# Transposing the normalised tokens on VectorE in the expert stage of a one-core Mamba and mixture-of-experts kernel

## The chip, the cores and the metric

The kernel runs on one core of one Trainium2 chip. The metric is device time in microseconds for one launch, the median of several runs. The core's engines are TensorE (matmuls and transposes, results in PSUM), VectorE, ScalarE and GpSimd (elementwise work), and SyncE, which issues the DMAs. Each engine works through its own list of instructions in order, and semaphores tie the lists together.

## What is computed

The input has 4 sequences of 1024 tokens with 128 channels in fp32. A Mamba block comes first (layer norm, projection, convolution, selective scan over 64 states, gate, output projection, residual), then a layer norm. Behind it stand four mixture-of-experts layers, and a last residual and layer norm:

```python
logits = jnp.einsum('bsh,he->bse', x, rw) + rb
vals, idx = jax.lax.top_k(softmax(logits), K)          # K = 2 of E = 4 experts
vals = vals / vals.sum(axis=-1, keepdims=True)
xhat = (x - mu) * rsqrt(var + EPS)
xe = xhat[None] * g[:, None, None, :] + b[:, None, None, :]
h = gelu(einsum('ebsh,ehf->ebsf', xe, w1) + b1)        # F = 512
y = einsum('ebsf,efh->ebsh', h, w2) + b2
out = sum over e of comb[e] * (x + y[e])
```

## The kernel before

The first part of the kernel is the Mamba block; its scan fills VectorE until about 1346 us. The expert stage follows. It computes all four experts for all tokens and weights them. Its unit is a group of GT = 4 tiles of 128 tokens. There are NG = 8 groups in a layer and NL = 4 layers, so 32 groups, numbered n = 0 to 31; g is the number within the layer, gp the parity that chooses one of two buffers.

Each engine has a function `step(layer, g, gp, new, more, scale, split)` that emits its work for one group, and `run_layers` calls it for each of the 32. The order within an engine is the order of the calls in its `step`:

- TensorE: `first(n, ., ., e)` computes the hidden block of expert e, 4 blocks of 3 matmuls with 512 columns (L1352), from `xhT`, the transposed normalised tokens, kept as an upper part and a remainder. It rotates over three PSUM banks, so the fourth block needs a bank that ScalarE's GELU has read. `second(n, ., e)` multiplies by w2, 32 matmuls (L1364). The order is first 0, first 1, second 0, `stage_xh(n + 1)` (four transposes of the next group's tokens into PSUM, L1331), first 2, second 1, first 3, second 2, second 3. In the last step of a layer `bias_of_offset` (L1340, 32 matmuls with one column) stands between first 0 and first 1; it waits for the last `add_expert` of the step before (semaphore `f_sum`), since its result goes to the same PSUM bank. The first step of a layer waits behind first 0 for all of the layer's split weights (`f_wp`).
- ScalarE: the GELUs of the four experts (L1109), and ahead of those of expert 2 `stage_norm(n + 2)`: it centres (L1083) and scales (L1089) the tokens of the group after next into `xhs`. It waits for VectorE's moments and for GpSimd's root.
- VectorE: `stage_moments(n + 2)` (L1418 to L1660), `start_sum(n)` (L1726), `add_expert` of expert 0 (L1736, reads PSUM), in the last layer `finish_moments(g - 1)` (it begins with L1762), `split_xh(n + 1)` (L1744 casts the transposed tokens from PSUM to `xhT`, L1746 takes the remainder), `stage_scores(n + 1)` (L1670 to L1677), in a layer's last step `add_bias`, `add_expert` of expert 1, in the last layer `finish_norm` (L1649), `stage_router(n + 1)` (L1682 to L1709), `add_expert` of expert 2, in the steps g = 2, 4, 6 and 7 of layers 0 to 2 `split_w1` (L1624, L1627, for the next layer), `sum_bias(n + 1)` (L1716, L1719), `add_expert` of expert 3.
- GpSimd: the root of the variances (L708), the products of `stage_scores` (L846), in the last layer the root for `finish_moments`, the exponents (L838, between VectorE's scores and its router), the weighted biases (L855, between VectorE's router and `sum_bias`).

Group 0's and group 1's tokens are transposed at other places than the rest; `begins` marks step 0.

Of the kernel before, what the change touches and what calls it, by code (L numbers as in the profile page):

```python
# [11 lines left out]
P = 128  # L12
# [28 lines left out]
GT = 4  # L41
# [3 lines left out]
def build(nc, x, vecs, chan, taps, a_log, ident, w_in, w_xproj, w_dt, w_out,  # L45
          router_w, router_b, ln_g, ln_b, w1, b1, w2, b2, out):
    fp32 = mybir.dt.float32
    bf16 = mybir.dt.bfloat16
    fp32r = mybir.dt.float32r
    ALU = mybir.AluOpType  # L50
# [13 lines left out]
    with ctx:  # L64
# [3 lines left out]
        def sem(name):  # L68
            return ctx.enter_context(nc.semaphore(name))
# [34 lines left out]
        at_, space, limit = [0], [arena], [ARENA]  # L104

        def shaped(v, shape):
            if len(shape) == 2:
                v = v.rearrange("p (a b) -> p a b", b=shape[1])
            elif len(shape) == 3:
                v = v.rearrange("p (a b c) -> p a b c", b=shape[1], c=shape[2])  # L110
            elif len(shape) == 4:
                v = v.rearrange("p (a b c d) -> p a b c d", b=shape[1], c=shape[2], d=shape[3])
            return v

        def carve(n):

            at_[0] += n
            assert at_[0] <= limit[0], at_[0]
            return space[0][:, at_[0] - n:at_[0]]

        def take(*shape):
            return shaped(carve(int(np.prod(shape))), shape)
# [29 lines left out]
        FRONT_END = at_[0]  # L152
# [84 lines left out]
        xhT = parts_xh[:].rearrange("p (g w t) -> p g w t", g=2, w=2)  # L237
# [6 lines left out]
        xhs = take(2, GT, P)  # L244
# [24 lines left out]
        b1_s = take(NL * E * GT)  # L269
        at_[0] = USZ_AT  # L270
        xsum_o = take(GT, H)
        at_[0] = BST_AT
        usz_last = take(2, HALVES, 2, TC)
        xres_last = carry[:, 0, 0:H]
# [87 lines left out]
        f_xhT = sem("f_xhT")  # L362
        f_xhTs = sem("f_xhTs")
# [15 lines left out]
        f_xhu = sem("f_xhu")  # L379
# [5 lines left out]
        f_xn = sem("f_xn")  # L385
# [11 lines left out]
        FIN0, LG0, XH0 = 1, 1, 1  # L397
# [101 lines left out]
        def xh_bank(n):  # L499
            return 4 if isinstance(n, int) and n == 0 else 5  # L500
# [621 lines left out]
        def _(pe):  # L1122
# [51 lines left out]
            for k in range(ITEMS):  # L1174
# [3 lines left out]
                for h in range(HALVES):  # L1178
                    last = nc.tensor.matmul(PS[0:N + R, 4 * bb, :], wx_s[:, h, 0:N + R], u_s[bb][:, h],
                                            start=(h == 0), stop=(h == 1))  # L1180
# [6 lines left out]
                for h in range(HALVES):  # L1187
                    last = nc.tensor.matmul(PS[:, 4 * bb + 2 + h, :], wdt_s[N:N + R, h * P:(h + 1) * P],
                                            dtr_s[bb][N:N + R, :], start=True, stop=True)
# [7 lines left out]
                for t in range(TT // P):  # L1197
                    for h in range(HALVES):
                        last = nc.tensor.matmul(PS[:, 4 * bb + 1, t * N:(t + 1) * N],
                                                u_s[bb][:, h, t * P:(t + 1) * P], wx_s[:, h, N + R:],  # L1200
                                                start=(h == 0), stop=(h == 1))
# [65 lines left out]
            def project(m):  # L1267

                pe.wait_ge(g_done, m + 1)
                if held(m) and not (isinstance(m, int) and m == NCH - 1):  # L1270
                    pe.wait_ge(post_done, m)
                for h in range(HALVES):
                    last = nc.tensor.matmul(projected(m), G[:, h], wout_s[:, h], start=(h == 0),
                                            stop=(h == 1 and in_end(m)))
                if not in_end(m):
                    for r in range(2):
                        last = nc.tensor.matmul(projected(m), ident_s[:], xres, start=False, stop=(r == 1))
                last.then_inc(out_ready, 1)
# [48 lines left out]
            def stage_xh(n, gp):  # L1327

                pe.wait_ge(f_xn, n + 1)
                for s in range(GT):  # L1330
                    last = nc.tensor.transpose(PS[:, xh_bank(n), s * P:(s + 1) * P], xhs[:, gp, s], ident_s[:])  # L1331
                last.then_inc(f_xhT, 1)
# [11 lines left out]
            def first(n, lp, gp, e):  # L1344


                for c in range(GT):
                    i = E * GT * n + GT * e + c

                    pe.wait_ge(f_gelu, i + (3 if e == c == 0 else 1))  # L1350
                    for part_w, part_x in ((0, 0), (0, 1), (1, 0)):
                        last = nc.tensor.matmul(PS[:, HIDDEN[(GT * e + c) % 3], :],  # L1352
                                                w1p[:, lp, part_w, e, c * P:(c + 1) * P],
                                                xhT[:, gp, part_x],
                                                start=(part_w + part_x == 0), stop=(part_w == 1))
                    last.then_inc(f_h, 1)
# [21 lines left out]
            def step(layer, g, gp, new, more, scale, split):  # L1378
                l, pair, lp = layer
                n = l * NG + g  # L1380
                starts = isinstance(g, int) and g == 0
                if starts:
                    pe.wait_ge(f_wp, l * E + 1)
                pe.wait_ge(f_xhTs, n + 1)
                first(n, lp, gp, 0)
                if starts:
                    pe.wait_ge(f_wp, l * E + E)
                if isinstance(n, int) and n == 0:
                    project(NCH - 1)
                if new:  # L1390
                    bias_of_offset(*new, n)
                begins = isinstance(n, int) and n == 0
                first(n, lp, gp, 1)
                second(n, lp, 0)
                if more and not begins:
                    stage_xh(n + 1, 1 - gp)
                first(n, lp, gp, 2)
                second(n, lp, 1)
                first(n, lp, gp, 3)
                if begins:  # L1400
                    stage_xh(1, 1)
                second(n, lp, 2)
                if isinstance(n, int) and n == 0:
                    pe.wait_ge(p_link, (NCH - 1) * P_LINKS + 1)
                if new:
                    pe.wait_ge(f_bias, new[0] + 1)
                second(n, lp, 3)

            run_layers(pe, begin, step)


        @block.vector
        def _(dve):
# [74 lines left out]
            for k in range(ITEMS):  # L1488
# [8 lines left out]
                for h in range(HALVES):  # L1497
                    last = nc.vector.tensor_scalar(rl[bb][:, h], PS[:, 4 * bb + 2 + h, :], chan_s[:, h, KC + 1:KC + 2],
                                                   0.0, ALU.add, ALU.max)
# [154 lines left out]
            def stage_moments(n, g):  # L1654

                dve.wait_ge(f_sum, E * n + E)
                if held(n):
                    dve.wait_ge(f_xn, n)
                moments(f_moments, n * 2, lambda s: at(X, g, s), st_f, mv_f, rs_f, GT, f_var)
                nc.vector.tensor_scalar(nm_f, mv_f[:, :, 0], -1.0, None, ALU.mult).then_inc(f_neg, 1)  # L1660
# [69 lines left out]
            def add_expert(n, g, gp, e):  # L1730
# [7 lines left out]
                                                          ALU.mult, ALU.add)  # L1738
                last.then_inc(f_sum, 1)

            def split_xh(n, gp):

                dve.wait_ge(f_xhT, n + 1 + XH0)
                nc.vector.tensor_copy(xhT[:, gp, 0], PS[:, xh_bank(n), :]).then_inc(f_xhu, 1)  # L1744
                dve.wait_ge(f_xhu, n + 1)
                nc.vector.tensor_tensor(xhT[:, gp, 1], PS[:, xh_bank(n), :], xhT[:, gp, 0].bitcast(fp32), ALU.subtract).then_inc(f_xhTs, 1)  # L1746
# [86 lines left out]
            def step(layer, g, gp, new, more, scale, split):  # L1833
                l, pair, lp = layer
                n = l * NG + g
                next_l, _, next_lp = new or layer
                if more:
                    stage_moments(n + 2, (g + 2) % NG)
                start_sum(n, g, gp)
                begins = isinstance(n, int) and n == 0  # L1840
                add_expert(n, g, gp, 0)
                if last_layer(l) and not (isinstance(g, int) and g == 0):
                    finish_moments(g - 1)
                if more:
                    if not begins:
                        split_xh(n + 1, 1 - gp)
                    stage_scores(n + 1, next_l)
                if new:
                    add_bias(next_l, next_lp)
                add_expert(n, g, gp, 1)  # L1850
                if last_layer(l) and not (isinstance(g, int) and g == 0):
                    finish_norm(g - 1, 1 - gp)
                if more:
                    stage_router(n + 1, 1 - gp)
                if begins:
                    split_xh(1, 1)
                add_expert(n, g, gp, 2)
                if split:
                    split_w1(*split)
                if more:  # L1860
                    sum_bias(n + 1)
                if not (last_layer(l) and isinstance(g, int) and g == NG - 1):
                    add_expert(n, g, gp, 3)
# [51 lines left out]
```

## Time and profile before

| | |
|---|---|
| Median of 3 runs | 2208.34 us (2207.08 to 2210.01) |
| The profiled execution | 2209.82 us, of which its span from first to last instruction is 2208.2 us |
| Granted TensorE clock, mean | 0.983 |
| Busy share of the span | TensorE 97%, its weight loads 58%, VectorE 83%, ScalarE 73%, GpSimd 42% |

The busy shares are means over the scan and the expert stage, in which different engines are busiest. The rows below come from one profiled execution; times in them are microseconds from the start of the span, and a duration called mean is in nanoseconds.

### The profile page before, as it was taken

What the parts mean: (1) busy time and instruction counts of PE and PEld (TensorE: products, weight loads), DVE (VectorE), ACT (ScalarE), POOL (GpSimd) and SP (SyncE); (2) the same over time, 40 slices, a digit from 0 to 9 for tenths busy, and PEclk for the clock granted to TensorE, in tenths of its full rate; (3) what the DMA queues carried; (4) which work ended last, traced back from release to release, by engine and by line L of the source; (5) the groups of instructions that cost most, each with busy time, mean ns of one, the idle gap of its engine ahead of it and who ended that gap; (6) DMA issues with size and microseconds to landing.
All of it is one profiled execution on the core that took longest, in us unless ns stands there. A gap on an engine that the chain in (4) does not pass through costs nothing.

```text
span 2208.2 us, 50669 instructions
## 1 busy us (share of the span) xinstructions
PE 2133.7 (97%) x17080; PEld 1270.6 (58%) x17080; DVE 1833.8 (83%) x2721; ACT 1617.4 (73%) x2160; POOL 926.1 (42%) x453
## 2 busy tenths in 40 slices
PE   7978999999999999999999998999999999999998
PEld 3432333333333333333333336899999999999997
DVE  6879999999999999999999997666565556556775
ACT  5878999999999999999999995445455455545453
POOL 3124344444444444444444333544444444444542
PEclk9978999999999999999999999999999999999999
DMA  5994212121212122222222134000100010000000
GB/s 172 299 281 133 49 41 48 40 48 40 48 40 47 40 47 42 45 44 44 45 42 46 41 86 149 1 0 0 39 1 0 0 39 1 0 1 2 14 10 15
DMA packets 354957, 114.93 MB, mean 52 GB/s; under 512 B 283000, under 2 KB 345600, under 8 KB 354624
## 3 DMA queue, kind: packets, MB, share of 16 engines
q1 hardware_dynamic: 350416, 110.92, 20.0%
q10 hardware_dynamic: 4464, 3.02, 0.4%
q8 instruction: 44, 0.72, 0.1%
q14 instruction: 33, 0.27, 0.0%
HBM read 67.98 MB, written 45.88 MB: 52 GB/s over the span
## 4 chain that ended last, share of the span: by engine, by line
PE 41%; DVE 29%; issue 23%; SPq 3%; ACT 2%; POOL 1%; DVEq 1%; DMA 0%; ACTq 0%; POOLq 0%
DVE arena L1588 25%; PE PS L1364 20%; PE PS L1352 16%; PE PS L1249 1%; ACT behind L981 1%; SPq L519 1%; SPq L615 1%; SPq L521 1%; PE PS L1232 1%; ACT behind L971 1%; PE PS L1331 1%; PE PS L1219 1%; PE PS L1340 1%; DVE arena L1431 0%; PE PS L1142 0%
## 5 line engine op out<-in xcount | busy, mean ns | idle before, releaser
L1588 DVE TENSOR_TENSOR_SCAN arena<-behind 128x1040 f32<-128x1040 f32 x512 | 1153.8, 2308 | 14.3 <-ACT behind L981 10.6
L1109 ACT ACTIVATE arena<-PS,arena 128x512 f32<-128x512 f32 x512 | 344.6, 688 | 405.8 <-PE PS L1352 405.3
L971 ACT ACTIVATE behind<-PS 128x1024 f32<-128x1024 f32 x512 | 526.4, 1028 | 100.7 <-DVE arena L1588 52.5
L1249 PE MATMUL PS<-arena 128*32 128x128 f32 x8192 | 566.2, 406 | 0.0
L981 ACT ACTIVATE behind<-PS 128x1024 f32<-128x1024 f32 x512 | 540.0, 1055 | 16.4 <-PE PS L1232 9.4
L1364 PEld LDWEIGHTS PS<-arena 128*128 128x128 f32 x4096 | 473.2, 192 | 7.7
L1364 PE MATMUL PS<-arena 128*128 128x128 f32 x4096 | 473.5, 275 | 0.0
L791 POOL COPY behind<-carry 128x64 f32<-128x64 f32 x128 | 212.9, 1664 | 508.2 <-ACT carry L998 266.8
L1249 PEld LDWEIGHTS PS<-arena 128*32 128x32 f32 x8192 | 234.9, 119 | 287.5 <-issue 211.3
L1352 PE MATMUL PS<-parts_xh,parts_w 128*128 128x512 f32 x1536 | 383.4, 401 | 9.5 <-ACT arena L1109 6.5
L1736 DVE SCALAR_TENSOR_TENSOR arena<-PS,arena 128x128 f32 (+1 forms) x508 | 142.8, 343 | 258.3 <-PE PS L1364 257.2
L1232 PE MATMUL PS<-arena 96*128 96x512 bf16 x1024 | 313.9, 389 | 42.0 <-ACT behind L981 14.3
L1352 PEld LDWEIGHTS PS<-parts_xh,parts_w 128*128 128x128 f32 x1536 | 284.2, 191 | 68.5 <-ACT arena L1109 10.3
L1219 PE MATMUL PS<-arena,Ast 96*128 96x512 bf16 x1024 | 313.9, 389 | 2.9 <-ACT behind L971 2.7
L1232 PEld LDWEIGHTS PS<-arena 96*128 96x128 bf16 x1024 | 68.8, 98 | 247.2 <-ACT behind L981 216.8
L1219 PEld LDWEIGHTS PS<-arena,Ast 96*128 96x128 bf16 x1024 | 58.7, 98 | 229.4 <-ACT behind L971 184.5
L838 POOL TENSOR_TENSOR arena<-euler,arena 128x16 f32<-128x16 f32 x32 | 92.6, 2895 | 166.1 <-DVE arena L1677 165.9
L846 POOL TENSOR_TENSOR arena<-arena 128x2048 f32<-128x2048 f32 x32 | 145.6, 4551 | 12.3 <-POOL arena L708 12.3
L855 POOL TENSOR_TENSOR arena<-arena 128x2048 f32<-128x2048 f32 x32 | 115.6, 3612 | 78.1 <-DVE arena L1707 78.1
L708 POOL TENSOR_TENSOR arena<-arena,neg_half 128x4 f32<-128x4 f32 (+1 forms) x50 | 50.7, 1014 | 226.7 <-DVE arena L1426 226.6
L805 POOL COPY arena<-arena 64x64 f32<-64x64 f32 x64 | 130.1, 2032 | 11.8 <-POOL behind L791 9.7
L717 POOL TENSOR_SCALAR arena<-arena 128x1 f32<-128x1 f32 x32 | 60.2, 1883 | 151.4 <-DVE arena L1562 151.4
(139 smaller groups left out, 1433.4 us busy)
## 6 DMA issues: line engine op xcount, KB each, us to landing
dl_d<-arena SPq DMA_DIRECT2D x48, 256.0 KB, 3.5
du_d<-arena SPq DMA_DIRECT2D x48, 256.0 KB, 3.5
arena<-dl_d SPq DMA_DIRECT2D x512, 24.0 KB
arena<-b_d SPq DMA_DIRECT2D x64, 192.0 KB
arena<-du_d SPq DMA_DIRECT2D x512, 24.0 KB
b_d<-arena SPq DMA_DIRECT2D x48, 128.0 KB, 2.4
u_d<-behind SPq DMA_DIRECT2D x8, 512.0 KB, 3.9
sz_d<-arena SPq DMA_DIRECT2D x8, 512.0 KB, 4.7
```

The source lines that it names most:

```text
L791: nc.gpsimd.tensor_copy(seg(dB[:, G_])[:, :, 0], carry[:, pair, d:d + GD]).then_inc(slot_ready, 1)
L846: nc.gpsimd.tensor_tensor(scored, X[:, bass.ds(g * GT, GT), :].unsqueeze(2).broadcast_to([P, GT, E, H]), rw_s[:, bass.ds(l, 1)].broadcast_ ...
L971: nc.scalar.activation(seg(dA[:, half])[:, :, 1:], PS[:, 0:2, :].rearrange("p j (i t) -> p (j i) t", t=TC), ACT.Exp).then_inc(exp_done, 1)
L981: nc.scalar.activation(seg(dB[:, G_])[:, :, 1 + 2 * OCT * r:1 + 2 * OCT * (r + 1)], PS[:, 2:4, :].rearrange("p o (t d) -> p d (o t)", d=GD ...
L1109: nc.scalar.activation(hT[:, e % 2, c], PS[:, HIDDEN[(GT * e + c) % 3], :], ACT.Gelu, bias=bias1[:, lp, e * GT + c:e * GT + c + 1]).then_i ...
L1219: last = nc.tensor.matmul(PS[:, j, :], Ast[0:ROWS, kk * (DB // GI) + 2 * q + j, :], rhs_d[kk][0:ROWS, 2 * q + j].rearrange("r i t -> r (i ...
L1232: last = nc.tensor.matmul(PS[:, 2 + oct_ % 2, :], Bst[kk][0:ROWS, oct_, :], rhs_u[kk][0:ROWS, oct_, :, G_ * GD:(G_ + 1) * GD], start=True, ...
L1249: last = nc.tensor.matmul(PS[32 * j:32 * j + 32, 4 + kk, 0:DB], cd[:, pair, j, 32 * i:32 * i + 32], seg(hb[kk])[:, :, 1 + 16 * j + i], sta ...
L1352: last = nc.tensor.matmul(PS[:, HIDDEN[(GT * e + c) % 3], :], w1p[:, lp, part_w, e, c * P:(c + 1) * P], xhT[:, gp, part_x], start=(part_w ...
L1364: last = nc.tensor.matmul(PS[:, y_bank(n, e, s), s * P:(s + 1) * P], hT[:, e % 2, c, s * P:(s + 1) * P], w2_s[lp][:, e * GT + c], start=(c ...
L1588: nc.vector.tensor_tensor_scan(hb[kk][:, q * QD * SEG:(q + 1) * QD * SEG], dA[:, q % 2], dB[:, G_, lo:lo + QD * SEG], 0.0, ALU.mult, ALU.a ...
L1736: last = nc.vector.scalar_tensor_tensor(at(X, g, s), PS[:, Y_BANK[e], s * P:(s + 1) * P], comb[:, gp, s * E + e:s * E + e + 1], at(X, g, s ...
```

## The change

In the expert stage the tokens of groups 2 to 31 are no longer transposed by TensorE. VectorE does it at the place where it has so far split the transposed tokens, in the step of the group before: 16 instructions, each of which takes 32 partitions and 4 x 32 elements, transposes the four 32x32 blocks in them and writes them to another set of 32 partitions of a new tile `xh_turned` in SBUF. The cast and the remainder then read that tile and not PSUM. The step's wait for ScalarE's normalised tokens (`f_xn`) moves from TensorE to VectorE. Groups 0 and 1 keep TensorE's transposes, and so does the code of `split_xh` for them.

```diff
         at_[0] = USZ_AT
         xsum_o = take(GT, H)
+        at_[0] = FRONT_END
+        xh_turned = take(GT, P)
...
                 second(n, lp, 0)
-                if more and not begins:
-                    stage_xh(n + 1, 1 - gp)
                 first(n, lp, gp, 2)
...
+            def turn_and_split(n, gp):
+
+                dve.wait_ge(f_xn, n + 1)
+                dve.wait_ge(f_xhTs, n)
+                for i in range(4):
+                    for j in range(4):
+                        last = nc.vector.transpose(xh_turned[32 * j:32 * j + 32, :, 32 * i:32 * i + 32],
+                                                   xhs[32 * i:32 * i + 32, gp, :, 32 * j:32 * j + 32])
+                last.then_inc(f_xhT, 1)
+                dve.wait_ge(f_xhT, n + 1 + XH0)
+                whole = xh_turned.rearrange("p s t -> p (s t)")
+                nc.vector.tensor_copy(xhT[:, gp, 0], whole).then_inc(f_xhu, 1)
+                dve.wait_ge(f_xhu, n + 1)
+                nc.vector.tensor_tensor(xhT[:, gp, 1], whole, xhT[:, gp, 0].bitcast(fp32), ALU.subtract).then_inc(f_xhTs, 1)
...
                     if not begins:
-                        split_xh(n + 1, 1 - gp)
+                        turn_and_split(n + 1, 1 - gp)
                     stage_scores(n + 1, next_l)
```

## Rows read from the trace of the kernel before

**Rows 1.** Chain that ended last, from 1330 us on: shares of lines.
```profile
by line: PE PS L1364 50.3%; PE PS L1352 39.6%; PE PS L1331 1.6%; PE PS L1340 1.3%; PE PS L1249 1.2%; issue 0.7%; POOL arena L838 0.7%; POOL arena L846 0.5%; POOL arena L855 0.4%; PE PS L1287 0.4%; POOL arena L708 0.3%; DVE arena L1418 0.3%;
```

**Rows 2.** Timeline of TensorE (PE), one group of layer 0: start, duration, instructions.
```profile
1444.62 3.73 PE L1364 MATMUL PS<-arena 128*128 128x128 f32 x32
1448.18 0.60 PE L1331 MATMUL PS<-ident_s,arena 128*128 128x128 f32 x4
...
1451.37 3.73 PE L1364 MATMUL PS<-arena 128*128 128x128 f32 x32
...
1457.68 7.30 PE L1364 MATMUL PS<-arena 128*128 128x128 f32 x64
1464.74 5.70 PE L1352 MATMUL PS<-parts_xh,parts_w 128*128 128x512 f32 x24
1470.28 3.73 PE L1364 MATMUL PS<-arena 128*128 128x128 f32 x32
```

**Rows 3.** Timeline of VectorE (DVE), the same stretch; in brackets idle time before.
```profile
1448.47 1.13 DVE L1736 SCALAR_TENSOR_TENSOR arena<-PS,arena 128x128 f32 x4 [4.78 <-PE PS L1364]
1449.51 0.68 DVE L1744 CAST parts_xh<-PS 128x512 fp32r<-128x512 f32 x1
...
1456.74 0.17 DVE L1682 TENSOR_REDUCE arena<-arena 128x4 f32<-128x16 f32 x1 [0.39 <-POOL arena L838]
...
1462.78 1.22 DVE L1716 TENSOR_TENSOR arena<-arena 128x1024 f32<-128x1024 f32 x1
...
1465.24 1.12 DVE L1736 SCALAR_TENSOR_TENSOR arena<-PS,arena 128x128 f32 x4 [0.51 <-PE PS L1364]
1466.28 0.86 DVE L1418 BATCH_NORM_STATS2 arena<-arena 128x6 f32 x4
...
1467.90 1.18 DVE L1726 SCALAR_TENSOR_TENSOR arena<-arena 128x128 f32 x4
```

**Rows 4.** Timeline of GpSimd (POOL), the same stretch.
```profile
1453.82 2.89 POOL L838 TENSOR_TENSOR arena<-euler,arena 128x16 f32<-128x16 f32 x1 [5.27 <-DVE arena L1677]
1459.14 3.61 POOL L855 TENSOR_TENSOR arena<-arena 128x2048 f32<-128x2048 f32 x1 [2.43 <-DVE arena L1707]
```

**Rows 5.** Groups of VectorE instructions (busy us, mean ns); L1624: shortest, median, longest ns.
```profile
L1418 DVE BATCH_NORM_STATS2 arena<-arena 128x6 f32 x92 | 19.8, 277 | 0.0
L1482 DVE TENSOR_TENSOR arena<-arena 128x128 f32<-128x128 f32 x1 | 0.3, 293 | 0.0
L1726 DVE SCALAR_TENSOR_TENSOR arena<-arena 128x128 f32 x92 | 26.4, 345 | 0.7 <-issue 0.3
L1624 DVE CAST parts_w<-arena x12: 415/422/672, 1436.7 to 1993.1; - x9, 128x512 fp32r<-128x512 f32 x3
```

**Rows 6.** Timelines of ScalarE (ACT) and TensorE in step 0.
```profile
1370.10 1.28 ACT L1083 ACTIVATE arena<-arena 128x128 f32<-128x128 f32 x4 [7.42 <-DVE arena L1660]
...
1373.31 1.65 PE L1352 MATMUL PS<-parts_xh,parts_w 128*128 128x512 f32 x3 [5.73 <-ACT arena L1109]
```

**Rows 7.** L1639's durations (shortest, median, longest ns), and GpSimd beside the longest.
```profile
L1639 DVE COPY arena<-arena x2: 228/1838/3447, 1350.5 to 1363.1; 128x128 f32<-128x128 f32 x2
...
1362.73 3.70 POOL L855 TENSOR_TENSOR arena<-arena 128x2048 f32<-128x2048 f32 x1 [2.59 <-DVE arena L1707]
```

**Rows 8.** Timelines of VectorE and TensorE at the end of layer 0.
```profile
1542.97 1.12 DVE L1736 SCALAR_TENSOR_TENSOR arena<-PS,arena 128x128 f32 x4
...
1544.81 4.42 PE L1340 MATMUL PS<-lb_s,arena 128*128 128x1 f32 x32
```

**Rows 9.** Last layer: L1762's durations, ends of two moments, GpSimd's products between.
```profile
L1762 DVE TENSOR_TENSOR arena<-arena x7: 680/1315/2256, 2031.5 to 2185.5; 128x512 f32 x6, 128x512 f32<-128x512 f32 x1
...
2077.40 0.16 DVE L1660 TENSOR_SCALAR arena<-arena 128x4 f32<-128x4 f32 x1
2103.41 0.16 DVE L1660 TENSOR_SCALAR arena<-arena 128x4 f32<-128x4 f32 x1
...
2079.03 4.58 POOL L846 TENSOR_TENSOR arena<-arena 128x2048 f32<-128x2048 f32 x1 [0.46 <-POOL arena L708]
```

## The prediction, made before the changed kernel was run

> **What bounds the kernel now.** I read the chain that ended last first, then the timelines of single groups in the expert stage. The stage runs from about 1346 us to the end, 32 groups in four layers, and the change touches nothing else. There the chain is TensorE almost alone: half of it in L1364, 40% in L1352, and the transposes of L1331 hold 1.6% [rows 1]. A group of layers 0 to 2 takes TensorE 25.66 us without a gap, 1444.62 to 1470.28 [rows 2]. So whatever leaves TensorE shortens the stage, as long as no other engine's loop over one group becomes longer than TensorE's.
>
> The second reading is VectorE's loop, because its order is fixed in `step`. Its idle time looks large (4.78 us before the first `add_expert` of a group, [rows 3]), but not all of it is free. Follow one round: first add 1448.47, then the split, the scores, GpSimd's exponent 1453.82 to 1456.71, router 1456.74, GpSimd's weighting to 1462.75, `sum_bias` 1462.78, last add 1465.24, moments until 1467.90 [rows 3, 4]. VectorE works in order, so it can't use its waits for GpSimd for what stands behind them. Whatever is put between the first add and the scores pushes all of this back, one for one.
>
> **What is removed.** TensorE loses four transposes in each of 30 groups. With them, second() and the first() behind it take 1444.62 to 1451.37, 6.75 us; without, 1451.37 to 1457.68, 6.31 us [rows 2]. 0.44 us a group, 30 x 0.44 = 13.2 us, all on the path; a group becomes 25.22 us. VectorE's cast now reads SBUF and not PSUM: 0.42 us by L1624 [rows 5] for the 0.68 of L1744 [rows 3], 0.26 less.
>
> **What is added: T.** Sixteen VectorE instructions of 32 partitions x 128 elements, in front of that cast. No row shows this operation. The nearest make one pass over 128 elements per partition. L1418: 277 ns each [rows 5], but four in 0.86 us [rows 3], so they overlap and follow at (0.86 - 0.277) / 3 = 0.195 us. L1482: 293 ns, and L1726: 345 ns [rows 5]. Bounds: all overlapped, T = 16 x 0.195 = 3.1 us; none overlapped, at the slowest row, T = 16 x 0.345 = 5.5. I take L1482's duration without overlap, T = 16 x 0.293 = 4.7 us: successive instructions go to other partitions here, so I don't count on the overlap of rows that stay on theirs.
>
> The Trainium skill ("VectorE: DVE Perf Modes", "Two Vector instructions with no wait between them") states that an instruction starts only when all earlier ones have finished if its output starts in another quadrant than the last output; here it does so every time. No row of this trace shows it. The same page ("The three transpose paths") gives 311 ns for a pass over 128 elements, by which T would be 5.0 us and the sum below some 6 us more (an estimate), and its rules send a 128x128 transpose to TensorE. It speaks against this change.
>
> **Where T lands in layers 0 to 2.** Times from t0, when TensorE begins first() of expert 2 (1448.18 in [rows 2]; there the transposes stand first). First add at +0.29; to the exponent 5.35 (1448.47 to 1453.82) less 0.26, plus T; to the router 2.92; router and weighting 6.04; `sum_bias` 1.95 (2.46 to the last add, less its 0.51 idle); last add and moments 2.66 [rows 3, 4]. Sum 18.95 + T = 23.65, against 25.22 to the next t0: moments end 1.57 us ahead of it. Their reader is ScalarE's normalisation, which stands in front of the GELUs of expert 2. Step 0 of this trace shows that chain failing: ScalarE, idle 7.42 us until VectorE's L1660, starts at 1370.10, and TensorE goes on at 1373.31 after 5.73 us idle [rows 6]. So TensorE's fourth hidden block needs the moments 3.3 us earlier, and it begins 2.1 us after t0 (three quarters of 2.8). Room: 1.57 + 2.1 - 3.3 = 0.4 us. An ordinary group still gains its 0.44.
>
> Two places have no room. (a) Four steps of a layer (g = 2, 4, 6, 7) run split_w1 behind the third add. Its cast copies from SBUF to SBUF, and such a copy waits out a GpSimd operation: L1639 ran 228 ns once and 3447 ns beside GpSimd's L855, which ended at 1362.73 + 3.70 = 1366.43 [rows 7]. VectorE now gets to that cast while L855 runs, so split_w1's 1.15 us fall behind it and into the loop: 0.4 - 1.15, a stall of 0.75 us in the step after g = 2 and after g = 4, 6 x 0.75. After g = 7 TensorE meets it earlier, at the wait for f_wp behind the next layer's first(0): it is there at 1464.74 - 1448.18 - 0.44 + 2.8 = 18.9 us after t0, the split ends at 18.95 + T - 1.95 - 2.66 + 1.15 = 20.2: 3 x 1.3. Together 8 us. (b) In a layer's last step TensorE's bias_of_offset waits for the last add of the step before. Now that add begins at 1542.97 and is over at 1544.0, and L1340 starts at 1544.81 [rows 8]. After, it is over at 18.95 + T - 1.62 (moments) + 1.15 = 23.2, and TensorE is there at 18.9 again. Stall 4.3 us, three times: 13 us. It takes in the stall after g = 6.
>
> **The last layer.** Here finish_moments stands in front of the split, and its L1762 reads two SBUF tiles while GpSimd's L846 runs: 680 ns at best, 2256 at worst [rows 9]. From moments to moments it is 2077.40 to 2103.41, 26.01 us [rows 9], longer than TensorE's 25.66 already. The idle time before the first add is not in this loop: it goes by L846, which ends at 2083.61, and L1762 behind it. So T counts whole: 26.01 - 0.26 + 4.7 = 30.45 us, 5.2 longer than 25.22. Moments end 1.6 us before t0 in step 25 and 3.6 behind it in step 26, where the stall is 3.6 + 3.3 - 2.1 = 4.8; then 5.2 in each of steps 27 to 30: 25.6 us. (Steps 24 and 31 have no such work.)
>
> The Trainium skill ("SBUF — State Buffer", "Reading the diagram") calls the port pair of VectorE and GpSimd an exclusive lock; L1639 and L1762 agree. If it did not bear on split_w1, the sum would be some 12 us less (8 of a, 3 x 1.15 of b; an estimate).
>
> **The sum.** -13.2 + 8 + 13 + 25.6 = +33.4 on this execution's 2209.8 (span 2208.2, 1.6 around it): 2243.2. It is 1.5 above the median of 2208.3, so I forecast **2242 us**, 1.5% slower.
>
> The ends. T = 3.1: no stall in (a), 3 x 2.7 in (b), last layer 1.7 + 4 x 3.6 = 16, sum -13 + 8 + 16 = +11, 2219. T = 5.5: nearly every step of layers 0 to 2 is short (some 13 us), 3 x 5.1 in (b), 5 x 6.0 in the last layer: +45, 2253. TensorE is slower behind a stall: three matmuls took 1.65 us after step 0's [rows 6], where twelve take 2.8 elsewhere. In the last layer VectorE's loop hides that; in (b) it can add some 1.5 us each, 5 in all, which I leave to the range.
>
> **Rivals.**
> 1. The sixteen overlap, T 3.1 to 4.2: 2219 to 2232. For it: small VectorE instructions without a wait between them overlap in this trace. Against: none of them changes its partitions.
> 2. They are slower than any row, since a transpose fills before it drains: 0.39 us each, T = 6.2. Then VectorE's loop without any wait for TensorE (1.18 start_sum + 18.66 + 6.2 = 26.0) is longer than 25.22 in layers 0 to 2 too: +60, 2268.
> 3. The other side, faster: T fits the slack. The point is T = 2.0: (b) 3 x 1.6, last layer some 10 us with its first two steps free, sum +1. At T = 1.3 (0.08 us each) (b) 2.7, last layer 5.6: -5, 2203. Against: even L1418, with overlap, follows at 0.195.
> 4. VectorE's loop in the last layer is not the bound and no bias stall comes: 2195 to 2200. Against it stands that 26.01 is measured and that L1762's wait grows.
>
> **Chances.** The forecast, T 4.2 to 5.5: 0.62. Rival 1: 0.18. Rival 2: 0.11. Rival 3: 0.05, half of it faster by over 0.2%. Rival 4: 0.04. A measurement of this kernel tells 0.2% (4.4 us) from no change. Faster 0.06, same 0.03, slower 0.91. The likeliest case alone gives 2230 to 2258 with the clock's 5 us; the range reaches down to T = 3.1 and up between T = 5.5 and 6.2: 2218 to 2264.
>
> **What would show it.** Right: only 8 of L1331's 128 left; a burst of sixteen that takes 4.2 to 5.5 us; 25.2 us a group in layers 0 to 2 where nothing stalls; TensorE idle before L1340 until VectorE's add, some 4 us, three times; in the last layer TensorE idle before L1352, released by ScalarE's L1109, some 5 us in five steps that last 30.4 us. Wrong: a burst under 2.1 or over 6 us; L1762 not held by L846; split_w1's cast not held by L855; or TensorE waiting for xhT itself, which in this account is ready some 9 us early, and 3 in the last layer.

## The result: 2264.5 us, 2.6% slower, half a microsecond above the forecast's range

The changed kernel takes 2264.47 us (median of 6 runs, 2263.41 to 2267.92) against 2209.11 for the kernel before (6 runs): a ratio of 1.0256, 95% interval 1.0243 to 1.0269. The forecast was 2242 us in a range of 2218 to 2264. The direction and each place of the loss came as said; the sum was 33 us where 55 came, and the measured time lies just outside the range.

The page of the changed kernel, its chain by engine and the group of the new instructions (busy us, mean ns):

```profile
PE 2144.5 (95%) x16960; PEld 1272.2 (56%) x16960; DVE 2013.3 (89%) x3201; ACT 1613.1 (71%) x2160; POOL 927.1 (41%) x453
DVE 37%; issue 36%; POOL 13%; PE 7%; SPq 3%; ACT 2%; DVEq 1%; DMA 0%; POOLq 0%; ACTq 0%
L1747 DVE STREAM_TRANSPOSE arena<-arena 32x128 f32<-32x128 f32 x480 | 145.9, 304 | 6.2
```

TensorE has 120 matmuls fewer, and its 41% of the chain of the kernel before has become 7%: the chain now runs through VectorE and the GpSimd operations that its loop waits for. ("issue" in the second row is time in which an engine waited for nothing that the profile shows.) The new instructions last 304 ns each. Line numbers of TensorE, ScalarE and GpSimd are two higher than before (L1354 is first(), L1366 second(), L1342 bias_of_offset, L848 and L857 GpSimd's products).

VectorE's timeline in step 27 of the changed kernel (last layer), and GpSimd's beside it, answer to [rows 3] and [rows 9]:

```profile
2118.65 0.16 DVE L1660 TENSOR_SCALAR arena<-arena 128x4 f32<-128x4 f32 x1
2118.81 1.14 DVE L1726 SCALAR_TENSOR_TENSOR arena<-arena 128x128 f32 x4
2120.15 1.12 DVE L1736 SCALAR_TENSOR_TENSOR arena<-PS,arena 128x128 f32 x4 [0.20 <-DVE arena L1726]
2121.19 4.18 DVE L1777 TENSOR_TENSOR arena<-arena 128x512 f32 x1
...
2126.92 5.08 DVE L1747 STREAM_TRANSPOSE arena<-arena 32x128 f32<-32x128 f32 x16
2132.04 0.43 DVE L1752 CAST parts_xh<-arena 128x512 fp32r<-128x512 f32 x1
```

```profile
2120.29 4.53 POOL L848 TENSOR_TENSOR arena<-arena 128x2048 f32<-128x2048 f32 x1 [0.46 <-POOL arena L710]
```

The reader is to see three things. The burst takes 5.08 us and is followed at 2132.04, so T is 5.1 and not 4.7. L1777, which was L1762, takes 4.18 us because it ends only behind L848 (2124.82). And VectorE no longer waits for TensorE before the first add: the row at 2120.15 has 0.20 us of idle time, and not behind TensorE, where the kernel before had 4.78 us in layer 0 ([rows 3]) and 2.65 us in a step of the last layer (before its row at 2107.48).

TensorE's timeline in the changed kernel, in steps 3 and 5, at the end of layer 0, in the step behind it, and in the last layer, in the order of time:

```profile
1451.30 0.97 PE L1354 MATMUL PS<-parts_xh,parts_w 128*128 128x512 f32 x3 [0.38 <-ACT arena L1111]
...
1503.06 0.97 PE L1354 MATMUL PS<-parts_xh,parts_w 128*128 128x512 f32 x3 [0.82 <-ACT arena L1111]
...
1550.04 6.96 PE L1342 MATMUL PS<-lb_s,arena 128*128 128x1 f32 x32 [4.59 <-DVE arena L1736]
1556.86 5.47 PE L1354 MATMUL PS<-parts_xh,parts_w 128*128 128x512 f32 x12
...
1586.30 3.06 PE L1354 MATMUL PS<-parts_xh,parts_w 128*128 128x512 f32 x12 [1.43 <-DVE parts_w L1627]
...
2091.43 1.65 PE L1354 MATMUL PS<-parts_xh,parts_w 128*128 128x512 f32 x3 [5.43 <-ACT arena L1111]
...
2100.09 7.30 PE L1366 MATMUL PS<-arena 128*128 128x128 f32 x64
...
2122.18 1.65 PE L1354 MATMUL PS<-parts_xh,parts_w 128*128 128x512 f32 x3 [3.70 <-ACT arena L1111]
...
2130.84 7.30 PE L1366 MATMUL PS<-arena 128*128 128x128 f32 x64
```

These are the stalls that the prediction named: at the fourth hidden block (0.38, 0.82, then 5.43 and 3.70 in the last layer), before bias_of_offset (4.59), and at the wait for the split weights (1.43). No stall of another kind appears in steps 2 to 31. The new thing is the length of the rows behind them: 6.96 us for the 32 narrow matmuls that took 4.42 in [rows 8], and 5.47 for twelve matmuls of first(). The windows of that stretch (length, then busy us and counts of TensorE, its weight loads, VectorE, ScalarE and GpSimd, then the granted clock, of which 1.00 is 2.4 GHz, then the DMA):

```profile
1545.00:1548.00 3.00, 0.45 (x2) 0.02 (x1) 2.75 (x3) 1.78 (x3) 0.77 (x1) 1.00 0.00 0
1548.00:1551.00 3.00, 0.96 (x5) 0.99 (x5) 2.81 (x13) 0.00 (x0) 0.00 (x0) 0.61 0.00 0
1551.00:1554.00 3.00, 3.00 (x16) 3.00 (x15) 1.48 (x10) 0.00 (x0) 2.28 (x2) 0.50 0.02 5
```

TensorE was idle from 1545.4 to 1550.0; the clock was granted at half, 1.2 GHz, from within that time on, and it stayed there through the narrow matmuls.

The kernel before had such a stretch too, without any idle time. Its windows of TensorE at the same place (length, busy us and count, granted clock), behind the 32 narrow matmuls of [rows 8]:

```profile
1547.00:1550.00 3.00, 3.00 (x15) 0.57 0.01 3
1550.00:1553.00 3.00, 3.00 (x8) 0.50 0.00 0
```

Measured by the start of each group's 64 matmuls of second(2) and second(3) in both traces, the 55.1 us divide as follows. The forecast's column is its own sum, with the 0.44 us of removed work counted where it falls.

| part | forecast | measured |
|---|---|---|
| steps 0 and 1 | -0.4 | +0.5 |
| 21 steps: 19 of layers 0 to 2 (without layer ends), and steps 24 and 25 | -1.2 | +2.9 |
| the three layer ends (39.42, 38.44, 39.34 us; before 32.46, 30.86, 29.27) | +11.7 | +24.6 |
| steps 26 to 30 (32.48, then 30.75 to 30.80 us; before 25.69) | +23.4 | +27.1 |
| sum | +33.4 | +55.1 |

### The profile page after: what moved, and what is told of

The parts are those of the page before. It is cut to its first block, busy times and chain, and to the rows that moved or that the text cites. A ratio compares the mean times of both kernels' runs of the same rounds, so it can differ in the third digit from the quotient of the medians.

```text
span 2263.3 us, 50927 instructions
## 1 busy us (share of the span) xinstructions
PE 2144.5 (95%) x16960; PEld 1272.2 (56%) x16960; DVE 2013.3 (89%) x3201; ACT 1613.1 (71%) x2160; POOL 927.1 (41%) x453
## 4 chain that ended last, share of the span: by engine, by line
DVE 37%; issue 36%; POOL 13%; PE 7%; SPq 3%; ACT 2%; DVEq 1%; DMA 0%; POOLq 0%; ACTq 0%
DVE arena L1588 25%; POOL arena L848 5%; POOL arena L840 4%; POOL arena L857 3%; PE PS L1366 2%; DVE arena L1736 2%; DVE arena L1716 2%; POOL arena L710 2%; DVE arena L1418 1%; DVE parts_w L1624 1%; PE PS L1251 1%; PE PS L1354 1%; ACT behind L983 1%; DVE arena L1777 1%; SPq L521 1%
## 5 line engine op out<-in xcount | busy, mean ns | idle before, releaser
L1111 ACT ACTIVATE arena<-PS,arena 128x512 f32<-128x512 f32 x512 | 338.6, 687 | 402.2 <-PE PS L1354 402.0
L1366 PEld LDWEIGHTS PS<-arena 128*128 128x128 f32 x4096 | 478.1, 194 | 8.5
L1366 PE MATMUL PS<-arena 128*128 128x128 f32 x4096 | 477.6, 277 | 0.0
L1354 PE MATMUL PS<-parts_xh,parts_w 128*128 128x512 f32 x1536 | 394.2, 407 | 38.7 <-ACT arena L1111 31.5
L1354 PEld LDWEIGHTS PS<-parts_xh,parts_w 128*128 128x128 f32 x1536 | 286.6, 193 | 104.5 <-ACT arena L1111 41.4
L1747 DVE STREAM_TRANSPOSE arena<-arena 32x128 f32<-32x128 f32 x480 | 145.9, 304 | 6.2
L848 POOL TENSOR_TENSOR arena<-arena 128x2048 f32<-128x2048 f32 x32 | 146.1, 4566 | 12.3 <-POOL arena L710 12.3
L857 POOL TENSOR_TENSOR arena<-arena 128x2048 f32<-128x2048 f32 x32 | 115.7, 3616 | 78.5 <-DVE arena L1707 78.5
```

The source lines that it names most:

```text
L848: nc.gpsimd.tensor_tensor(scored, X[:, bass.ds(g * GT, GT), :].unsqueeze(2).broadcast_to([P, GT, E, H]), rw_s[:, bass.ds(l, 1)].broadcast_ ...
L1111: nc.scalar.activation(hT[:, e % 2, c], PS[:, HIDDEN[(GT * e + c) % 3], :], ACT.Gelu, bias=bias1[:, lp, e * GT + c:e * GT + c + 1]).then_i ...
L1366: last = nc.tensor.matmul(PS[:, y_bank(n, e, s), s * P:(s + 1) * P], hT[:, e % 2, c, s * P:(s + 1) * P], w2_s[lp][:, e * GT + c], start=(c ...
```

## The experiments

Two theories stood against each other after the result. Theory A: all is VectorE's loop, as predicted, with T = 5.1, and the rest of the difference is TensorE's lowered clock behind the stalls. Theory B: the transposes cost something of their own (they disturb GpSimd, or the idle time before bias_of_offset is the whole loss there). Each kernel below is the changed one with the edit shown, unless it says otherwise, and is timed beside the kernel before.

**Removal alone.** All transposes left out; cast and remainder take the tokens as they are.

```diff
-                for i in range(4):
-                    for j in range(4):
-                        last = nc.vector.transpose(...)
-                last.then_inc(f_xhT, 1)
-                dve.wait_ge(f_xhT, n + 1 + XH0)
-                whole = xh_turned.rearrange("p s t -> p (s t)")
+                dve.sem_inc(f_xhT, 1)
+                whole = xhs[:, gp].rearrange("p s t -> p (s t)")
```

> The changed kernel with no transposes at all from group 2 on: cast and remainder take the normalised tokens as they are, so the experts see untransposed data. It is the removal alone. Theory: every group 0.44 us shorter on TensorE, nothing stalls: 30 x 0.44 = 13 us, time 2195 to 2197. Rival (the last layer's loop of 25.8 us is the bound there): 2199 or more.

Measured: 2196.70 us against 2210.86, ratio 0.9933 (0.9917 to 0.9950). TensorE's steps alternate between 25.21 and 25.43 us in layers 0 to 2 and are all of 25.21 to 25.24 us in the last. The layer ends take 32.0, 30.4 and 32.0 us with no idle time in them. The removed work is worth 14 us, if nothing replaces it; the 13.2 of the forecast holds.

**Addition alone.** The kernel before, with the sixteen added ahead of `split_xh` and TensorE's transposes kept.

```diff
+                        turn_too(n + 1, 1 - gp)
                         split_xh(n + 1, 1 - gp)
```

> The kernel before with the sixteen VectorE transposes added at the same place, their results unused; TensorE's transposes stay and are used. It is the addition alone. Theory: the last layer and the three bias stalls go by VectorE, so the kept TensorE work costs only in the steps of layers 0 to 2 without a stall, about 17 x 0.44: 2268 to 2273. Rival (the sums simply add): 2264.5 + 13 = 2278.

Measured: 2271.22 us, ratio 1.0275 (1.0258 to 1.0292). The two halves do not add: +60.4 and -14.2 would give 46, and both together gave 55. Where VectorE sets the pace, TensorE's removed work buys nothing. (The cast still reads PSUM here, so VectorE's loop is also some 0.26 us longer than in the changed kernel.)

**Half of the burst.** Eight transposes instead of sixteen; half of the tile is stale.

```diff
-                for i in range(4):
+                for i in range(2):
```

> The changed kernel with only eight of the sixteen transposes, so half of the tile is stale and the experts see wrong tokens there. T = 2.55 us. Theory (everything goes by VectorE's loop): no stall at the fourth hidden block in layers 0 to 2, 2.0 us of idle time at each of the three bias_of_offset with some 3 us of clock loss behind each, last-layer groups of 28.2 us; sum -13 + 6 + 10 + 12.5, time 2220 to 2227. Rival (the loss is not proportional to T but comes with the transposes as such): above 2235.

Measured: 2221.45 us, ratio 1.0057 (1.0040 to 1.0073), with 2.06 us of idle time before each bias_of_offset. Inside theory A's band. With half of T the kernel is 12 us slower than the kernel before and with all of it 55: the slack takes the first part.

**Partitions that do not change.** Sixteen transposes of the same size, all from partitions 0 to 31 to partitions 0 to 31; the cast takes the tokens as they are.

```diff
-                        last = nc.vector.transpose(xh_turned[32 * j:32 * j + 32, :, 32 * i:32 * i + 32],
-                                                   xhs[32 * i:32 * i + 32, gp, :, 32 * j:32 * j + 32])
+                        last = nc.vector.transpose(xh_same[0:32, i, :, 32 * j:32 * j + 32],
+                                                   xhs[0:32, gp, :, 32 * j:32 * j + 32])
```

> The changed kernel with all sixteen transposes reading partitions 0 to 31 and writing partitions 0 to 31, at sixteen places of a larger tile; the cast takes the tokens as they are, so the experts see untransposed data. Same count, same size, only the partitions no longer change. Theory (instructions follow without overlap because the partitions change): the burst shrinks from 5.1 us to about 3.1 (0.2 us each), and the time to about 2232. Rival (a transpose is not overlapped whatever its partitions): burst 5.1 us, time 2262 to 2266.

Measured: 2236.28 us, ratio 1.0111 (1.0091 to 1.0130). VectorE's timeline and the group, in this kernel:

```profile
1451.24 3.19 DVE L1748 STREAM_TRANSPOSE arena<-arena 32x128 f32<-32x128 f32 x16
L1748 DVE STREAM_TRANSPOSE arena<-arena 32x128 f32<-32x128 f32 x480 | 95.8, 261 | 0.0
```

(3.19 - 0.26) / 15 = 0.195 us from one to the next, the figure that the prediction has for L1418, where the changed kernel has (5.06 - 0.30) / 15 = 0.317. The time, 2236.28 us, is 4 us above the theory's 2232. So the rule of the Trainium skill on instructions whose quadrant changes ("VectorE: DVE Perf Modes", "Two Vector instructions with no wait between them") is borne out here: the change of partitions costs 0.12 us for each of the sixteen, and 28 us of the kernel. In this kernel input and output both stay. Which of the two matters is seen in the changed kernel, whose first four transposes of a burst (i = 0) all read partitions 0 to 31 and write to four different sets:

```profile
1450.32 1.25 DVE L1747 STREAM_TRANSPOSE arena<-arena 32x128 f32<-32x128 f32 x4
```

(1.25 - 0.30) / 3 = 0.317 us again, with only the output's partitions changing. So the output's change alone is enough; whether the input's alone would be is not shown. The layer ends of the kernel on fixed partitions take 37.9 us with 2.7 us of idle time: less 25.2 and 3.6 (the narrow matmuls at the full clock), 6.4 us are lost to the clock there, no less than behind the longer stall.

**The last layer by TensorE.** `stage_xh` and `split_xh` come back in the last layer.

```diff
+                if more and isinstance(l, int) and l == NL - 1:
+                    stage_xh(n + 1, 1 - gp)
...
-                        turn_and_split(n + 1, 1 - gp)
+                        (split_xh if last_layer(l) else turn_and_split)(n + 1, 1 - gp)
```

> The changed kernel, but in the last layer TensorE transposes again, as in the kernel before. Theory: the last layer's part of the loss (27 us by its periods of 30.8 us in five steps) goes, except 1 to 2 us because VectorE enters it without slack; time 2237 to 2241. Rival (the last layer is only where a lag from before is paid): above 2250.

Measured: 2237.92 us, ratio 1.0123 (1.0106 to 1.0140): 26.6 us less than the changed kernel. The last layer's loss is its own and no lag from before.

**finish_moments behind the transposes.** In the last layer the two change places.

```diff
+                if more and not begins:
+                    turn_and_split(n + 1, 1 - gp)
                 if last_layer(l) and not (isinstance(g, int) and g == 0):
                     finish_moments(g - 1)
                 if more:
-                    if not begins:
-                        turn_and_split(n + 1, 1 - gp)
```

> The changed kernel with the order of two parts turned round in the last layer: transposes, cast and remainder first, then finish_moments. Theory (L1762's successor, two SBUF inputs, is held until GpSimd's L848 ends; the transposes are not): the transposes run beside L848, finish_moments' first instruction takes 0.7 us and not 4.2, and a last-layer group takes 27.3 us and not 30.8; time about 2248. Rival (the transposes are held too, or GpSimd is slowed by them): groups stay near 30.8, 2262 or more.

Measured: 2245.88 us, ratio 1.0159 (1.0142 to 1.0176), and steps 26 to 30 of 27.26 to 27.61 us. VectorE in such a step, and GpSimd beside it:

```profile
2114.46 5.06 DVE L1747 STREAM_TRANSPOSE arena<-arena 32x128 f32<-32x128 f32 x16
2119.55 0.43 DVE L1752 CAST parts_xh<-arena 128x512 fp32r<-128x512 f32 x1
2120.01 0.69 DVE L1754 TENSOR_TENSOR parts_xh<-arena,parts_xh 128x512 fp32r<-128x512 f32 x1
2120.62 0.69 DVE L1777 TENSOR_TENSOR arena<-arena 128x512 f32 x1
```

```profile
2113.56 4.53 POOL L848 TENSOR_TENSOR arena<-arena 128x2048 f32<-128x2048 f32 x1 [0.46 <-POOL arena L710]
```

L1777, now behind the end of L848 (2118.09), takes 0.69 us instead of 4.18, and the burst keeps its 5.06 and L848 its 4.53: a transpose runs beside GpSimd's L848, an operation with two SBUF inputs does not. The order alone was worth 18.6 us.

**The idle time filled.** 19 matmuls of 512 columns ahead of bias_of_offset, results unused.

```diff
                 if new:
+                    for _ in range(19):
+                        nc.tensor.matmul(PS[:, 5, :], w1p[:, lp, 0, 0, 0:P], xhT[:, gp, 0], start=True, stop=True)
                     bias_of_offset(*new, n)
```

> The changed kernel with 19 extra matmuls of 512 columns on TensorE, into the free bank 5, ahead of bias_of_offset in the last steps of layers 0 to 2 (their results are not used). They fill 4.4 of the 4.6 us that TensorE idles there, three times. Theory (the lowered TensorE clock behind this idle time is what makes these steps 25 us longer in all and not 12): L1342 shrinks from 6.96 us to about 3.6, first() behind it from 5.5 to 3 to 5, and the time from 2264.5 to about 2253. Rival (the stall itself is the whole loss, or the 32 narrow matmuls lower the clock by themselves): unchanged, within 3 us.

Measured: 2257.27 us, ratio 1.0217 (1.0200 to 1.0234), 7.2 us less than the changed kernel and neither expectation: more than the rival's 3, less than the theory's 12. TensorE's timeline:

```profile
1543.48 4.47 PE L1394 MATMUL PS<-parts_xh,parts_w 128*128 128x512 f32 x19
1548.23 5.30 PE L1342 MATMUL PS<-lb_s,arena 128*128 128x1 f32 x32 [0.29 <-DVE arena L1738]
1553.40 4.62 PE L1354 MATMUL PS<-parts_xh,parts_w 128*128 128x512 f32 x12
```

The clock still falls, but only once the narrow matmuls run: it is granted in full until 1550 and at half from 1551, and they take 5.30 us for 6.96. The three layer ends take 36.9 us; less 25.2, 4.5 for the added matmuls, 0.3 idle and 3.6, some 3.3 us are still lost. The kernel before and the removal alone lost up to 3.2 us in the same way, with no idle time. So there are two causes, the idle time and the narrow matmuls, which the next run takes apart.

**One narrow pair instead of sixteen.** bias_of_offset computes one column, so later layers' biases are wrong; the wait stays.

```diff
-                for ec in range(E * GT):
+                for ec in range(E * GT - 1, E * GT):
```

> The changed kernel with one of the sixteen columns of bias_of_offset computed instead of all, so the later layers' first bias is wrong; the wait for VectorE's last add stays. Theory (the clock loss at a layer's end has two parts, the idle time and the 32 narrow matmuls behind it): idle 4.6 us as before, about 1.7 us lost behind it as in the last layer, so a step of 31.5 us and not 39; time about 2242. Rival (the idle time alone causes all 5.6 us of clock loss): steps of 35.5 us, time about 2254.

Measured: 2245.70 us, ratio 1.0162 (1.0146 to 1.0179), with layer ends of 32.70, 33.29 and 31.86 us. TensorE's timeline:

```profile
1549.16 0.56 PE L1342 MATMUL PS<-lb_s,arena 128*128 128x1 f32 x2 [4.58 <-DVE arena L1736]
1549.58 5.21 PE L1354 MATMUL PS<-parts_xh,parts_w 128*128 128x512 f32 x12
```

The mean is 32.6; less 25.2 for a step, 4.6 idle and some 0.3 for the pair, 2.5 us are lost to the clock behind the idle time alone. With all 32 narrow matmuls it is 39.1 - 25.2 - 4.6 - 3.6 (their length at the full clock, row below) = 5.7 us. The split that the theory made holds, but both its sizes were too small: 2.5 us where it said 1.7 (1.8 to 3.2 in the three ends), and 2245.7 us where it said 2242.

**Ahead of the first add.** The sixteen move to a function `turn_xh`, called before `add_expert` of expert 0; cast and remainder stay.

```diff
+                if more and not begins:
+                    turn_xh(n + 1, 1 - gp)
                 add_expert(n, g, gp, 0)
```

> The changed kernel with the same sixteen transposes moved ahead of the group's first add_expert, behind start_sum, in all layers; cast and remainder stay where they are. Theory (VectorE's idle time there is real in layers 0 to 2, some 6 us, and in the last layer the transposes run beside GpSimd's L848 while L1762's successor has to wait for it anyway): no stalls in layers 0 to 2, last-layer groups of 27.4 us from the point where the slack is used up, 6 us lost; time 2200 to 2205, faster than the kernel before. Rival (a transpose is held off by GpSimd's L848 like L1639 was): the first add is 3 to 4 us later in every group, stalls come back in all layers, 2225 or more.

Measured: 2205.91 us, ratio 0.9979 (0.9970 to 0.9989): slightly faster than the kernel before, and 58.6 us faster than the change as made. The idle time of VectorE before the first add was real slack. It does not make the transposes free: against the removal alone, 2196.70 us, they still cost 9 to 11 us (by the medians, or by each kernel's difference to the kernel before beside it), in the last layer and at the end of layer 0. VectorE's and GpSimd's timelines, in the last layer and at the end of layer 0:

```profile
1536.20 1.13 DVE L1736 SCALAR_TENSOR_TENSOR arena<-PS,arena 128x128 f32 x4
1537.24 2.64 DVE L1624 CAST parts_w<-arena  x1
...
2100.67 5.08 DVE L1747 STREAM_TRANSPOSE arena<-arena 32x128 f32<-32x128 f32 x16
2105.77 1.12 DVE L1736 SCALAR_TENSOR_TENSOR arena<-PS,arena 128x128 f32 x4
2106.82 0.68 DVE L1780 TENSOR_TENSOR arena<-arena 128x512 f32 x1
```

```profile
1535.99 3.61 POOL L857 TENSOR_TENSOR arena<-arena 128x2048 f32<-128x2048 f32 x1 [2.43 <-DVE arena L1707]
...
2101.05 4.55 POOL L848 TENSOR_TENSOR arena<-arena 128x2048 f32<-128x2048 f32 x1 [0.43 <-POOL arena L710]
```

The burst lies over L848 and is not held. The time is 0.9 us above the expected 2200 to 2205, and a loss that the theory did not have stands at 1537.24: in layer 0 split_w1's cast is held by L857 (2.64 us for 0.42), and TensorE idles 2.50 us before bias_of_offset there; that step takes 36.4 us, where the removal alone has 32.0.

**Two versions from this.** The first keeps TensorE's transposes in the last layer; the second also puts split_w1 of g = 2, 4 and 6 behind the last add.

```diff
-                if split:
+                if split and new:
                     split_w1(*split)
...
                     add_expert(n, g, gp, 3)
+                if split and not new:
+                    split_w1(*split)
```

> The sixteen transposes ahead of the first add_expert in layers 0 to 2, TensorE's transposes in the last layer. Theory: the last layer's five steps lose 4.9 us less to VectorE's loop and 3.1 us more to TensorE's transposes, and the stall ahead of bias_of_offset in layer 0 stays: 2203 to 2206, faster than the kernel before by 0.2 to 0.3%. Rival (last-layer stalls come back because VectorE enters it late): above 2207.

> As e9_best, and split_w1 of the steps g = 2, 4 and 6 stands behind the last add_expert and not ahead of sum_bias. Theory: its cast was held by GpSimd's L857 in layer 0 (2.64 us for 0.42) and made TensorE idle 2.5 us ahead of bias_of_offset with the clock lowered behind it; without it that step is 32.0 us or less and not 36.4: 2198 to 2202. Rival (the split costs the same wherever it stands): no difference from e9_best.

Measured: 2204.81 us, ratio 0.9981 (0.9972 to 0.9990), and 2203.47 us, ratio 0.9969 (0.9958 to 0.9980). Both are faster than the kernel before. The first lies in its expected range. The second missed its 2198 to 2202; it has the lowest time of the versions that leave nothing out, 0.3% below the kernel before, but its 1.3 us to the first version lie within the spread of both (2201.5 to 2209.8, 2199.3 to 2205.2 us). (One of its eight executions took 6227 us, which nothing here explains; the ratio leaves it out, and without it the median is 2202.93.) Its trace shows that the move did something: the end of layer 0 fell from 36.4 to 34.2 us, and not to 32, since 1.91 us of idle time stayed there. In its layer 1 TensorE's row is that of the narrow matmuls at the full clock:

```profile
1756.64 3.63 PE L1342 MATMUL PS<-lb_s,arena 128*128 128x1 f32 x32
```

Of the 13 to 14 us that the removal is worth, the best version keeps 6 to 7: the last layer keeps its TensorE transposes, and the end of layer 0 its stall.

## Why the prediction was right on the mechanism and short on the sum

- *Removed: 13.2 us.* Right: 14.2 by the removal alone.
- *T = 4.7 us.* Too small. The term took L1482's 293 ns without overlap. Measured are 304 ns and a step of 0.317, T = 5.1. (The 311 ns that the prediction quotes from the Trainium skill stand there for a bf16 tile of 128x128; these are fp32 instructions on 32 partitions.) That there would be no overlap was right, and the run on fixed partitions shows why. Put into the prediction's own formulas, 5.1 for 4.7 adds 0.4 in six steps and three weight waits (3.6), about 1 in the three bias stalls, and makes the last layer 28.2 for 25.6: 7 us in all.
- *An ordinary group of layers 0 to 2 gains its 0.44.* At the edge at T = 5.1: the room of 0.4 us is used up. Some ordinary steps stall for 0.2 us (0.24 in step 2, 0.17 in step 10), and steps 2, 10 and 18 take 25.74, 25.67 and 25.50 us where the removal alone has 25.2.
- *(a) split_w1 held by GpSimd.* Right. The six steps behind g = 2 and g = 4 stall for 0.4 to 0.9 us (the rows at 1451.30 and 1503.06 are two of them; 0.75 forecast), the three weight waits are 1.43 us (1.3 forecast). L1624 in the changed kernel, beside its 415/422/672 ns of [rows 5]:

```profile
L1624 DVE CAST parts_w<-arena x12: 2634/2645/2787, 1439.9 to 2023.0; - x9, 128x512 fp32r<-128x512 f32 x3
```

- *(b) 4.3 us before bias_of_offset, three times.* The idle time was right, 4.6. **The failed step is what stands behind it**: "in (b) it can add some 1.5 us each, 5 in all, which I leave to the range". It added 12: the three layer ends lose 5.7 us each to the clock (17 us), where the kernel before lost 4.7 in all (3.2, 1.6 and 0 us: 92.6 us for its three ends, less 3 x 25.7 and 3 x 3.6). The term was left out of the sum and sized by three wide matmuls, not by the 32 narrow ones that follow here. The trace of the kernel before already showed the clock at half around them (the windows from 1547 on, above).
- *The last layer, 30.45 us a group.* Right: 30.75 to 30.80, the difference being T. There the clock loss is hidden, as said, except in the first stalled step, whose 32.48 us hold 1.7 of it.
- 7 us of T, 12 of the clock and 2 of that step make 21 of the 22 us missing. The other microsecond lies in the first two steps and was not looked into.
- *Rivals.* Full overlap (1) is ruled out by the burst's 5.06 us, and what it would have given is measured by the fixed partitions, 2236 us, with clock losses at the layer ends as large (6.4 us each) that its 2219 to 2232 had not counted. (2) is nearest in time, with another cause: T was 5.1 and not 6.2. (3) and (4) fall with the burst and with L1777's 4.18 us.

## What to carry to other kernels

Work moved to an engine with idle time costs what the engine's in-order loop says, not what its idle share says: find the wait that stands idle for a producer that is itself the bound (here before the first add) and put the work ahead of that one. Against the kernel with no transposes, the sixteen cost 68 to 70 us behind the first add and 9 to 11 us ahead of it. And count a TensorE stall with what follows it: the matmuls behind it run at the lowered clock, and with 32 narrow ones there 4.6 us of idle time cost 10.3.

## What the runs showed of the hardware that was not expected

- A VectorE transpose of 32 partitions x 128 fp32 elements takes 304 ns and follows the last at 0.317 us when its output's partitions change; it takes 259 to 261 ns and follows at 0.195 us when neither input nor output changes.
- It runs beside a GpSimd operation on SBUF without either being longer (5.06 and 4.53 us, or 5.08 and 4.55), while a two-input operation and a cast, both from SBUF to SBUF, wait it out (4.18 us for 0.69, 2.64 for 0.42).
- 4.6 us of TensorE idle time cost 2.5 us more behind it, and 5.7 us where 32 narrow matmuls follow. The narrow matmuls alone, with TensorE busy throughout, were followed by the half clock as well: 3.2, 1.6 and 0 us lost at the three layer ends of the kernel before.
